# Two-layer graph network on one core: the flag's branch ahead of the last four tiles, whole evictions in twelve blocks, and normalization of more chunks by ScalarE

## What is computed

```
h = relu(layernorm(x))
h = relu(h @ enc_w1.T + b1) @ enc_w2.T + b2
for w in conv_w (5 rounds):
    agg = segment_sum((h @ w)[src], dst)
    r, z, n = GRU gates of (agg, h);  h = (1 - z) * n + z * h
x = x + sigmoid(decoder(relu(h)))
h = relu(layernorm(x))
v = normalized adjacency (1/sqrt of both degrees)
x = x + spmm(relu(spmm(h) @ W1.T + b1)) @ W2.T + b2
```

## Time and profile before

| what | value |
|---|---|
| median of 3 runs | 745.32 us |
| the profiled execution's own time | 745.62 us |
| its span, first to last instruction | 743.3 us |
| PE / DVE / ACT / POOL busy, share of the span | 97% / 45% / 42% / 6% |
| mean granted TensorE clock | 0.999 |
| PE busy in the first 18.6 us of 40 equal slices, then | 0.6, 0.8, 0.8, and 0.9 or more from the fourth to the 39th |

### The profile page before, as it was taken

One profiled execution on the slowest core, in us unless ns is written; L12 is line 12 of the kernel. 1 busy time (PEld: TensorE's weight loads), 2 busy tenths in 40 slices (PEclk: granted clock), 3 DMA queues, 4 the chain that ended last, 5 costly groups with the idle time before them and its releaser, 6 DMA issues.

```text
span 743.3 us, 9918 instructions
## 1 busy us (share of the span) xinstructions
PE 721.4 (97%) x4071; PEld 394.4 (53%) x4071; DVE 335.2 (45%) x677; ACT 315.2 (42%) x463; POOL 44.5 (6%) x56
## 2 busy tenths in 40 slices
PE   6889999999999999999999999999999999999997
PEld 3556666445444444444444444444445545558886
DVE  7999999525023241123231223646644631123432
ACT  3977877645344344234452334432447421212000
POOL 4240000000000000000000000120002210000000
PEclk9999999999999999999999999999999999999999
DMA  5020000734102332022230212710002000000100
GB/s 164 6 84 16 4 2 5 147 69 81 9 1 55 63 51 46 1 48 39 53 75 0 49 37 38 115 63 2 1 0 97 9 1 1 1 1 6 34 31 25
DMA packets 79240, 28.41 MB, mean 38 GB/s; under 512 B 70519, under 2 KB 78390, under 8 KB 79062
## 3 DMA queue, kind: packets, MB, share of 16 engines
q1 hardware_dynamic: 78230, 26.93, 17.2%
q0 software_dynamic: 240, 0.66, 0.3%
q10 hardware_dynamic: 720, 0.13, 0.1%
HBM read 8.03 MB, written 2.60 MB: 14 GB/s over the span
## 4 chain that ended last, share of the span: by engine, by line
PE 85%; DVE 9%; ACT 2%; DMA 2%; POOL 1%; issue 1%; SPq 0%; DVEq 0%; ACTq 0%; POOLq 0%
PE PSA L1241 35%; PE PSA L1458 9%; PE PSA L1323 7%; PE PSA L1402 5%; PE PSA L1186 4%; PE PSA L1254 3%; PE PSA L1263 3%; PE PSA L1258 3%; PE PSA L1262 3%; PE PSA L1256 3%; PE PSA L1265 3%; DVE CT L869 3%; PE PSA L1390 2%; PE PSA L1378 1%; DMA H<-yS 1%; DVE stat L834 1%
## 5 line engine op out<-in xcount | busy, mean ns | idle before, releaser
L1241 PE MATMUL PSA<-AT,H 128*128 128x512 fp8e3 (+1 forms) x1470 | 275.8, 347 | 0.8 <-DMA H<-yS 0.8
L1241 PEld LDWEIGHTS PSA<-AT,H 128*128 128x128 f16 x1470 | 126.8, 98 | 151.9 <-issue 12.0
L1078 DVE SCALAR_TENSOR_TENSOR rS<-PSA,bias,rS 128x512 f32<-128x512 f32 (+1 forms) x35 | 23.9, 682 | 261.6 <-ACT rS L1635 261.6
L1635 ACT ACTIVATE rS<-PSA,bias 128x512 f32<-128x512 f32 (+1 forms) x35 | 22.1, 632 | 199.6 <-PE PSA L1262 199.6
L869 DVE TENSOR_TENSOR CT<-CT 128x2048 bf16<-128x2048 bf16 x80 | 91.4, 1206 | 0.0
L1565 ACT ACTIVATE AT<-PSA 128x1000 fp8e3<-128x1000 f32 (+1 forms) x79 | 74.4, 997 | 20.7 <-PE PSA L1186 20.5
L1539 ACT ACTIVATE CTL<-AT 128x3125 fp8e3<-128x3125 fp8e3 (+1 forms) x25 | 69.9, 2797 | 0.0
L1402 PE MATMUL PSA<-CT,H 128*128 128x512 fp8e3 (+1 forms) x336 | 65.5, 351 | 0.3 <-POOL H L762 0.3
L1458 PE MATMUL PSA<-AT,CT 128*128 128x256 f16 x576 | 65.1, 273 | 0.6 <-DVE AT L1040 0.6
L1458 PEld LDWEIGHTS PSA<-AT,CT 128*128 128x128 fp8e3 x576 | 55.4, 98 | 7.2 <-DVE AT L1040 0.8
L1323 PE MATMUL PSA<-AT,H 128*128 128x512 fp8e3 x245 | 58.0, 379 | 1.2 <-ACT AT L1565 1.2
(11 more groups left out here) (181 smaller groups left out, 661.8 us busy)
## 6 DMA issues: line engine op xcount, KB each, us to landing
AT<-scale_scratch SPq DMA_DIRECT2D x1, 1562.5 KB, 6.5
H<-in_x SPq DMA_DIRECT2D x1, 1536.0 KB
out<-AT SPq DMA_DIRECT2D x12, 128.0 KB
comb_scratch<-CT SPq DMA_DIRECT2D x1, 960.0 KB, 4.5
comb<-comb_scratch SPq DMA_DIRECT2D x5, 192.0 KB, 2.5
H<-yS SPq DMA_TRANSPOSE x48, 2.5
H<-in_x SPq DMA_DIRECT2D x1, 512.0 KB, 4.9
CT<-AT SPq DMA_TRANSPOSE x25, 4.0
```

The costliest lines, as they stand in the source:

```text
L1241: last = nc.tensor.matmul(bank[:, 0:w], H16[:, l % 2, t, h, :], AT3[:, t, n0:n0 + w], start=(t == 0 and h == 0), stop=(t == T - 1))
```

## The change

There are five edits.

1. **The end.** The last four tiles (FLAGGED = 20 to 23) of PE and DVE move behind the wait for the flag and the branch, into both of its arms. In the arm for the flag that is not set (a new Else) nothing else stands; it lies behind the general version's code. SP, ACT and POOL are as before.
2. **Whole evictions.** In blocks 0 to 11 (WHOLE = 12) ACT waits for both halves of a block and evicts 2000 columns with one instruction, which frees both halves.
3. **Normalization.** Chunks 3, 4, 5 and 6 are normalized by ACT, each in the block ahead of its transposes and behind that block's encoder pieces; DVE has the small `shifts` in place of the four instructions. Only chunk 2 stays with DVE.
4. **Parts.** In blocks 12 and 13 PE does four matmuls of chunk 0 in each, where it did eight of chunk 0 and eight of chunk 1; what is left out stands in blocks 15 to 22.
5. **The start.** POOL numbers 128 lanes in f32, and ACT spreads them to the paired 16-bit table which POOL made before. The second of two matmuls at the start that feed nothing has 256 columns in place of 384. The semaphore `mhalf_set` is merged into `steps_set`.

```diff
         kf = early([PW, KW, SL], F32)
+        lanes = tf[:, KW - 1, :]
...
         CHECKED = 4
+        FLAGGED = 20
...
         REST = 7
+        WHOLE = 12
+        BY_SCALAR = (0, 1, 3, 4, 5, 6)
+        BY_VECTOR = (2,)
...
-        PART = {7: [(0, 0, 4)], 8: [(0, 4, 8)], 10: [(0, 8, 12)], 12: [(0, 12, 16)], 13: [(1, 0, 4)], 14: [(0, 16, 20)],
-                15: [(1, 4, 8)], 16: [(0, 20, 24)], 17: [(1, 8, 11)], 18: [(0, 24, T), (1, 11, 13)]}
-        PART.update({19 + i: [(1, 13 + 3 * i, 16 + 3 * i)] for i in range(4)})
+        PART = {7: [(0, 0, 4)], 8: [(0, 4, 8)], 10: [(0, 8, 12)], 12: [(0, 12, 14)], 13: [(0, 14, 16)], 14: [(0, 16, 20)],
+                15: [(1, 0, 4)], 16: [(0, 20, 24)], 17: [(1, 4, 8)], 18: [(0, 24, T), (1, 8, 11)]}
+        PART.update({19: [(1, 11, 14)], 20: [(1, 14, 18)], 21: [(1, 18, 21)], 22: [(1, 21, T)]})
...
-            pool.memset(mhalf[:, :], -0.5).then_inc(mhalf_set, 1)
+            pool.memset(mhalf[:, :], -0.5).then_inc(steps_set, 1)
...
-            pool.iota(iotaP, [[1, 128], [0, 2]], base=0, channel_multiplier=0,
-                      allow_small_or_imprecise_dtypes=True).then_inc(onehot_iotas, 1)
+            pool.iota(lanes, [[1, 128]], base=0, channel_multiplier=0,
+                      allow_small_or_imprecise_dtypes=True).then_inc(lanes_numbered, 1)
...
                     if b == block_of[2 * n_] - 1:
-                        normalized(n_)
+                        shifts(n_) if n_ in BY_SCALAR else normalized(n_)
...
+            def output_tile(u):
+
+                bank = PS[TILES[u % STARTED]]
+                dve.wait_ge(sum2_ready, u + 1)
+                link(nc.vector.scalar_tensor_tensor(OUT[:, u, :], bank[:, 0:F], dinvO[:, u:u + 1], X32[:, u, :],
+                                                    ALU.mult, ALU.add))
+                nc.vector.scalar_tensor_tensor(OUT[:, u, :], bank[:, F:2 * F], dinvO[:, u:u + 1], OUT[:, u, :],
+                                               ALU.mult, ALU.add).then_inc(output_ready, 1)
...
-                for u in range(2 * FG):
-                    bank = PS[TILES[u % STARTED]]
-                    dve.wait_ge(sum2_ready, u + 1)
-                    link(nc.vector.scalar_tensor_tensor(OUT[:, u, :], bank[:, 0:F], dinvO[:, u:u + 1], X32[:, u, :],
-                                                        ALU.mult, ALU.add))
-                    nc.vector.scalar_tensor_tensor(OUT[:, u, :], bank[:, F:2 * F], dinvO[:, u:u + 1], OUT[:, u, :],
-                                                   ALU.mult, ALU.add).then_inc(output_ready, 1)
+                for u in range(FLAGGED):
+                    output_tile(u)
...
             dve.wait_ge(flag_ready, 1)
+            chained = n[0]
             with dve.If(dve.value_load(flag[0:1, 0:1], min_val=0, max_val=1000) > 0):
+                for u in range(FLAGGED, 2 * FG):
+                    output_tile(u)
                 general_vector(dve)
+            n[0] = chained
+            with dve.Else():
+                for u in range(FLAGGED, 2 * FG):
+                    output_tile(u)
...
             pe.wait_ge(window_starts, 1)
-            for n in (512, 384):
+            for n in (512, 256):
...
-                    pe.wait_ge(tile_normalized, s + 1) if s < 2 else pe.wait_ge(later_normalized, s - 1)
+                    if s in BY_SCALAR:
+                        pe.wait_ge(tile_normalized, BY_SCALAR.index(s) + 1)
+                    else:
+                        pe.wait_ge(later_normalized, BY_VECTOR.index(s) + 1)
...
-            for u in range(STARTED, 2 * FG):
+            def next_tile(u):
+
                 pe.wait_ge(output_ready, u - STARTED + 1)
                 tile_sum(u, 0, 24)
                 tile_ends(u)
+
+            for u in range(STARTED, FLAGGED):
+                next_tile(u)
...
             pe.wait_ge(flag_ready, 1)
             with pe.If(pe.value_load(flag[0:1, 0:1], min_val=0, max_val=1000) > 0):
+                for u in range(FLAGGED, 2 * FG):
+                    next_tile(u)
                 general_tensor(pe)
+            with pe.Else():
+                for u in range(FLAGGED, 2 * FG):
+                    next_tile(u)
...
             def windows(b):
 
-                for g, gw in enumerate(groups(b)):
+                if b < WHOLE:
+                    act.wait_ge(windows_counted, 2 * b + 2)
+                    counts = PSA[0:P, 2:6, :].rearrange("p b (w c) -> p (b w) c", c=128)
+                    nc.scalar.activation(
+                        AT3[0:P, :, b * J * W:(b + 1) * J * W].rearrange("p t (w d) -> p t w d", w=J),
+                        counts[:, :, 0:W * T].rearrange("p w (t d) -> p t w d", t=T),
+                        ACT.Copy, saturate=False).then_inc(window_bank_free, 2)
+                for g, gw in enumerate(groups(b) if b >= WHOLE else []):
                     w0 = b * J + g * GW
                     act.wait_ge(windows_counted, 2 * b + g + 1)
                     counts = PSA[0:P, 2 + 2 * g:4 + 2 * g, :].rearrange("p b (w c) -> p (b w) c", c=128)
...
-                act.wait_ge(shifts_ready, s + 1)
+                act.wait_ge(shifts_ready, BY_SCALAR.index(s) + 1)
...
-            act.wait_ge(mhalf_set, 1)
+            act.wait_ge(steps_set, 3)
             nc.scalar.activation(flag_f[0:1, 0:1], mhalf[0:1, 0:1], ACT.Copy)
             for d, v in ((enc1, enc_w1T), (enc2, enc_w2T), (bias[:, 4:5], enc_b1), (bias[:, 5:6], enc_b2)):
                 act.dma_start(d, v).then_inc(encoder_loaded, 16)
+            act.wait_ge(lanes_numbered, 1)
+            nc.scalar.activation(iotaP, lanes.unsqueeze(2).to_broadcast([SL, 128, 2]), ACT.Copy).then_inc(onehot_iotas, 1)
...
                     encoder(step(b))
+                for s in BY_SCALAR[2:]:
+                    if b == block_of[2 * s] - 1:
+                        normalized(s)
                 if b in COMB:
```

More of the change, by code:

```diff
@@ L271, in gnn_kernel @@
         keys_ready = sem("keys_ready"); keys_transposed = sem("keys_transposed")
-        keys_copied = sem("keys_copied"); onehot_iotas = sem("onehot_iotas")
+        keys_copied = sem("keys_copied"); onehot_iotas = sem("onehot_iotas"); lanes_numbered = sem("lanes_numbered")
         onehots_ready = sem("onehots_ready"); windows_counted = sem("windows_counted")
@@ L276, in gnn_kernel @@
         ident_set = sem("ident_set"); gate_biases = sem("gate_biases")
-        mhalf_set = sem("mhalf_set"); weights_loaded = sem("weights_loaded"); combined_loaded = sem("combined_loaded"); encoder_loaded = sem("encoder_loaded")
+        weights_loaded = sem("weights_loaded"); combined_loaded = sem("combined_loaded"); encoder_loaded = sem("encoder_loaded")
         weights2_loaded = sem("weights2_loaded"); x_loaded = [sem("x_loaded0"), sem("x_loaded1")]; x_reloaded = sem("x_reloaded")
@@ L732, in _ @@
             gathered(1)
-            pool.wait_ge(mhalf_set, 1)
+            pool.wait_ge(steps_set, 3)
             roots(0)
```

## The result

| | before | changed |
|---|---|---|
| median of 5 runs | 745.32 us | 748.95 us |
| all runs | 744.95 to 745.64 | 748.48 to 750.28 |
| profiled execution, span | 745.62, 743.3 | 748.95, 746.8 |

The ratio is 1.005, with a 95% interval of 1.0039 to 1.0062. The changed kernel is slower by 3.6 us, twice the 1.8 of the forecast; the time lies inside the range, close to its upper end.

What follows compares the result with a forecast made beforehand. PE's own work, 85% of the path, was taken as the bound. The profiled 745.6 + 0.7 (build) - 0.1 (start) + 1.2 (branch, both ends) gave 747.4, so 747.1 as median; range 744.4 to 749.2 us.

Steps and rivals of the forecast that it cites:

- The end, gained: -1.6: Behind the last tile: DVE's drain at 743.0 no longer ends the span, SP's at 741.4 is late next; 1.6 us gained.
- The branch, paid: +2.8: Ahead of tile 20: PE's sequencer stands in the moved branch, and the uncovered gap of 2.8 us goes to the end.
- Rival A: At PE's moved branch: PE isn't held, so the sum is -1.0 us, 744.3; chance 11%.
- rival C: Last four tiles: the clock falls in PE's gap and they begin at the low level; +1.9 us, 749.0; chance 8%.
- The build: +0.7: Build blocks: the loop through ACT's normalization costs +2.1 us, and chunk 1's part in block 13 loses its 1.4 wait.
- the loop: Build, from chunk 4's transposes: each chunk's transposes wait for ACT's normalization; rounds of 8.6 and 7.5 us, together +2.1.
- the term of the whole evictions: Early build blocks: one 2000-column eviction takes 1.85 us against 1.90 for two overlapping; 0.05 to 0.1 us a block saved.
- The start: -0.1: PE's first counts: with 128 columns less they begin when DVE's first compare lets them; -0.1 us, between 0 and -0.3.
- B: Build: ACT has slack enough and the loop doesn't bind; build -1.5 us, whole -0.4, 744.9; chance 20%.
- D: PE's Else arm: it runs over the end of what was fetched, a second fetch; up to 3.7 us more, 750.8; chance 7%.

Runs made afterwards that it cites:

- the fall-through kernel: Kernel before with PE's branch ahead of tile 20 and its condition turned, so the last four tiles directly follow the branch; DVE's branch moved too: 743.13 us, ratio 0.9975.
- the first experiment: Kernel before with only the branch moved ahead of tile 20, on both PE and DVE: 747.37 us, ratio 1.0024, nine runs in two groups.

## Why the prediction was right and wrong

- **The end, gained: -1.6.** Right: 1.66 in the changed kernel, 1.7 with DVE's branch alone. From the last store's issue to the end it is 2.2 us, as forecast (2.3). SP is what is late next; with DVE's branch alone, PE's stands only 0.2 ahead of it.
- **The branch, paid: +2.8.** Right, in size and in kind. A row behind the end of the work gave the price of the same instruction in the middle of it, to a tenth. Rival A falls with the fall-through kernel: 86 ns where the jump isn't taken. The Trainium skill, "Runtime: NRT & Kernel Launch", section on instruction fetch mechanics, says that a taken branch forces a fetch when its target isn't in the current window of two pages, and that a page is 16 KiB, 256 instructions; the pair of 86 and 3751 ns agrees with that. I had judged by the 128 KiB for PE that the section also gives, by which PE would not pay; the 3718 ns decide against that figure, while a window of two pages, 512 instructions, is less than the 650 jumped over.
- **What failed.** The step is rival C, which I gave 8% and left outside the sum: "the clock falls in PE's gap". It came together with the forecast, in all five runs of the changed kernel as their times and their mean clock have it (the one of 750.28, at 0.989, seems to have had more than one fall), and cost 1.6 (I gave it 1.9, from tiles of the same length at half speed for 3.8 us; it lasted 3.4). The mistake was to treat it as another way in which things could go. It was a consequence of the forecast's own main term. Once I held that PE would stand for 2.6 us with its array empty, the question was what the clock does in such a pause. Rows 3 and 10 bounded it from both sides, at 1.5 and about 3, and a value so near to the upper bound deserved, as I judge it now, a half, not a twelfth. With half of 1.6 in the sum it would have been 747.9; with all of it, 748.7.
- **The build: +0.7.** Right in sign, near in size, and that by luck: two terms were wrong and nearly cancelled. Chunks 4, 5 and 6 came at 44.89, 53.66 and 61.27, where I had 44.6, 53.2 and 60.7, and each round of the loop took 8.8 and 7.6 for 8.6 and 7.5. But my loop was worked out for normalization alone, with whole evictions as a small gain, and the kernel with normalization and parts and no whole evictions shows what that costs: chunk 4 0.4 earlier than before, rounds of 8.3 and 7.1, chunk 6 only 1.0 later (59.61), not 2.1, and with the 1.6 that came back behind it the first gate product 0.6 earlier, not 0.7 later. So the loop exists, but its cost at chunk 6 was half of what I had. The step that failed beside it is the term of the whole evictions, 0.05 to 0.1 us a block gained. The time of one was right (1840 ns), but the waiting for two halves was not in it: PE stands 0.7 us in front of windows whose banks ACT frees at once and late. The runs put this edit at +0.5 alone and at +1.8 in the changed build. Without it the build and the start would have gained 0.8 to 1.
- **The start: -0.1.** It gave about -0.3 to -0.4, the end of my range or a little over it. The build and the start together are +1.05 at the first gate product, for +0.6 forecast. On the way to tile 19 a further 0.3 came back in the rounds. By the pages the sums there waited 0.8 us for transposed data before (L1241) and 0.4 after (L1260), and this is the scatter between traces named above rather than an effect of the edits.
- **Rivals B and D.** The changed build did not gain, so B's time did not come. But without the whole evictions it gains 0.6 us at the first gate product, although ACT is as full as the row said, so for these two edits B's sign was right. No second fetch was seen (D): there is one gap.

As a sum for the profiled execution: -1.66 + 2.8 + 1.6 + 0.74 = 3.5, against -1.6 + 2.8 + 0.6 = 1.8.

**Open.** Why the clock falls in some executions and not in others. All runs of the changed kernel had it, five of nine of the first experiment, eight of ten with the pause two tiles later. The pauses in the three traces are alike (2.6 to 2.7 us of idle array), and the early record goes with either outcome. Nor is it shown how much shorter a pause would have to be. That the low clock is what separates the two groups of the first experiment rests on the mean clock and the time of each run and on two traces, not on a trace of each run. And the pause ahead of PE's last tiles is not the only thing that brings such runs: three of ten with the other edits without the branch, and one of ten with the normalization on ACT alone, are 1.4 to 1.9 us over their medians at a lower mean clock, with PE's branch at the end. None of the 20 runs with normalization and parts but no whole evictions is, and none of the kernel before.

## What to carry to other kernels

A sequencer's wait behind the end of the work shows in the profile before, and has its full price once it is moved ahead of work on the bounding engine; lay the arm that runs right behind the branch, and the far jump stays at the end. When an edit makes a pause in TensorE's work, put the clock behind the pause into the sum, not among the rivals. And test the parts of a bundle: this one held 2.8 us of gain, and two edits that turned it into a loss of 3.6.

## What the hardware showed

- A taken jump over the general version holds PE's sequencer for 3.4 to 3.9 us in all kernels here (3391 to 3871 ns); the same branch not taken takes 86 ns.
- A pause of PE of 2.6 to 2.7 us of idle time can bring the granted clock from 2.4 to 1.2 GHz. The lower level began 0.2 us after PE started again in one trace and before PE started in the other (it is there from 735.2, PE starts at 735.61). It lasted 3.4 us in both, with PE busy to its end. Pauses of 1.80 us in the build, at the full level, did not do it, and one of 2.70 in the trace of the first experiment did not either.
- In the changed kernel the clock was still at the full level when the span ended, 3 us after the last matmul; in the kernel before it was down at that distance.
- Ahead of the first record of the clock (at 17.9 us in the kernel before) the view prints 1.00, but the matmuls there take as long as at the lower level: 1.86 us for sixteen of the windows, 1.11 later.
- One ScalarE copy of 2000 columns across four PSUM banks takes 1840 ns, and one of 1000 takes 1018. By these two the fixed part is 0.2 us, so twelve blocks could save 2.4 at most; the edit that saves it cost 0.5 alone and 1.8 in the changed build.
